# Query chunks with a deferred inversion, ten weight staging buffers, and reordered first tiles in a one-core graph transformer layer

## The reference

```
xn = layernorm(x)
deg = segment_sum(1, dst);  dinv = rsqrt(deg)
gnn = relu(segment_sum((xn @ W)[src] * dinv[src] * dinv[dst], dst) + b)
Q, K, V = xn @ Wq.T + bq, xn @ Wk.T + bk, xn @ Wv.T + bv     # 16 heads of 64
phiQ, phiK = elu(Q) + 1, elu(K) + 1
S = phiK^T V;  Z = sum(phiK)                                  # per head
mix = (phiQ S) / (phiQ Z + 1e-6) @ Wo.T + bo
x = x + gnn + mix
h = silu(xn2 @ w1.T * s1) * (xn2 @ w2.T * s2);  two gelu layers;  x = x + h @ w3.T * s3
```

## Time and profile before

| | |
|---|---|
| median of 3 runs | 1139.36 us (1137.54 to 1141.56) |
| the profiled execution | time 1137.78 us, span 1135.7 us |
| busy: PE, PEld, DVE, ACT, POOL | 1025.6, 853.8, 585.6, 289.7, 165.7 us |
| chain that ended last | PE 61%, DVE 17%, DMA 9%, ACT 4%, issue 4%, POOL 3% |
| mean granted TensorE clock | 0.953 |

### The profile page before, as it was taken

How to read it: one execution, slowest core, us unless ns; L and a number is a source line. 1 busy time by engine, 2 the same in 40 slices (tenths; PEclk the granted TensorE clock), 3 DMA queues, 4 the chain that set the end, 5 groups by cost and what they waited for, 6 DMA issues and landing times.

```text
span 1135.7 us, 13213 instructions
## 1 busy us (share of the span) xinstructions
PE 1025.6 (90%) x4932; PEld 853.8 (75%) x4932; DVE 585.6 (52%) x1074; ACT 289.7 (26%) x532; POOL 165.7 (15%) x208
## 2 busy tenths in 40 slices
PE   3779999998998979978989999788999997999998
PEld 2657888886878967856867785565877897999886
DVE  4766678666764776776137315752156510113354
ACT  5465213122124122121122113422013410125400
POOL 6010001001002013013040001000060005126200
PEclk9979999998998988987989999898999998999999
DMA  7120213102011012112335205643263201002043
GB/s 238 40 70 28 54 38 90 25 15 89 25 41 60 23 42 79 45 42 79 120 107 176 90 1 179 223 158 108 100 192 113 97 1 46 29 19 70 6 167 140
DMA packets 49405, 92.58 MB, mean 82 GB/s; under 512 B 16676, under 2 KB 20112, under 8 KB 49320
## 3 DMA queue, kind: packets, MB, share of 16 engines
q1 hardware_dynamic: 41640, 66.32, 17.7%
q0 software_dynamic: 7680, 25.17, 7.2%
HBM read 67.22 MB, written 23.76 MB: 80 GB/s over the span
## 4 chain that ended last, share of the span: by engine, by line
PE 61%; DVE 17%; DMA 9%; ACT 4%; issue 4%; POOL 3%; SPq 0%; DVEq 0%; POOLq 0%; ACTq 0%
PE PS L1198 8%; PE PS L1199 8%; PE PS L1200 8%; PE PS L1310 5%; PE PS L1311 5%; PE PS L1312 5%; DVE rec L1035 4%; PE PS L1237 3%; PE PS L1385 2%; PE PS L1384 2%; PE PS L1383 2%; POOL ring L355 2%; DMA phin_d<-phiq 2%; PE PS L1436 2%; PE PS L1437 2%
## 5 line engine op out<-in xcount | busy, mean ns | idle before, releaser
L1198 PE MATMUL PS<-ring,act_t 128*128 128x512 f32 (+1 forms) x480 | 199.6, 416 | 7.7 <-POOL ring L355 7.7
L1199 PE MATMUL PS<-ring,act_t 128*128 128x512 f32 (+1 forms) x480 | 193.5, 403 | 0.0
L1200 PE MATMUL PS<-ring,act_t 128*128 128x512 f32 (+1 forms) x480 | 193.4, 403 | 0.0
L1310 PE MATMUL PS<-act_t,ring 128*128 128x416 f32 (+1 forms) x432 | 163.7, 379 | 15.1 <-POOL ring L355 15.1
L1311 PE MATMUL PS<-act_t,ring 128*128 128x416 f32 (+1 forms) x432 | 155.0, 359 | 0.0
L1312 PE MATMUL PS<-act_t,ring 128*128 128x416 f32 (+1 forms) x432 | 154.2, 357 | 0.0
L1198 PEld LDWEIGHTS PS<-ring,act_t 128*128 128x128 f32 (+1 forms) x480 | 91.6, 191 | 33.6 <-POOL ring L355 11.8
L355 POOL TENSOR_TENSOR ring<-stage,ring 128x512 fp32r<-128x512 f32 x66 | 88.1, 1335 | 192.9 <-ACT ring L618 182.6
L1200 PEld LDWEIGHTS PS<-ring,act_t 128*128 128x128 f32 (+1 forms) x480 | 91.4, 190 | 23.5
L1199 PEld LDWEIGHTS PS<-ring,act_t 128*128 128x128 f32 (+1 forms) x480 | 91.8, 191 | 21.7 <-issue 0.9
L1310 PEld LDWEIGHTS PS<-act_t,ring 128*128 128x128 f32 x432 | 83.2, 192 | 24.5 <-POOL ring L355 20.1
(11 more groups left out here) (168 smaller groups left out, 1582.4 us busy)
## 6 DMA issues: line engine op xcount, KB each, us to landing
stage<-in_wslices_dram POOLq DMA_DIRECT2D x96, 256.0 KB, 2.9
xr<-x_d SPq DMA_DIRECT2D x27, 256.0 KB, 3.1
ctu<-ct_d SPq DMA_DIRECT2D x20, 320.0 KB, 3.2
phin_d<-phiq SPq DMA_DIRECT2D x8, 625.0 KB, 3.2
xrow<-in_x_dram SPq DMA_DIRECT2D x9, 512.0 KB, 3.5
xh<-in_x_dram SPq DMA_DIRECT2D x18, 256.0 KB, 2.5
x_d<-xh SPq DMA_DIRECT2D x18, 256.0 KB, 2.1
x_d<-xr SPq DMA_DIRECT2D x18, 256.0 KB, 2.1
```

The costliest lines, as they stand in the source:

```text
L1198: pe.matmul(out_ap, node_rows(0, k, t), ring[:, slot(k0 + k), 0, :], start=(k == 0), stop=False)
L1199: pe.matmul(out_ap, node_rows(1, k, t), ring[:, slot(k0 + k), 0, :], start=False, stop=False)
L1200: ins = pe.matmul(out_ap, node_rows(0, k, t), ring[:, slot(k0 + k), 1, :], start=False, stop=(k == KD - 1))
L1310: pe.matmul(out_ap, w[0], x_t[:, 0, k, o:o + n], start=(k == 0), stop=False)
```

## The change

It makes these edits:

- Six more staging buffers, `stage_x`, in memory that `wo_sb` and `ph_in` use later. Slices below 64 go round ten buffers, those from 64 on round four. SP waits until slice 63 is done before it loads `wo_sb`.
- The first two tiles: ScalarE takes the root of the second right behind the split of the first, and VectorE does the first tile's low part ahead of the second's inverse. `ln_finish` has one operation less, and its operations have one tensor input.
- Three windows in each of steps 10 to 36, and none after. `count_tile` moves behind the low halves of the weights. The sums of step 39 and the z units come after the first query unit, on TensorE and on ScalarE.
- Query chunks: the exp is written in place over `qmin`, `phiq` has three buffers, ScalarE reads the denominator out of PSUM and adds the constant (`den_copy`), TensorE does the denominator of chunk i-2, and VectorE's work is cut into `q_min`, `den_invert` (chunk i-3), `q_add` and `den_apply` (chunk i-3).
- `mix` waits for all 24 low parts of `ph` in place of 16.

```diff
-STAGE = 4
+PHI_BUFS = 3
+STAGE_A = 10
+STAGE_B = 4
...
-    u += [("z", i) for i in range(2)]
-    u += [("q", f, c) for f in range(KD) for c in range(3)]
+    u += [("q", 0, 0), ("z", 0), ("z", 1)]
+    u += [("q", f, c) for f in range(KD) for c in range(3) if f or c]
...
-    if 10 <= step < 40:
-        g, j = divmod(step - 10, 3)
-        return list(range(8 * g + 3 * j, 8 * g + min(3 * j + 3, 8)))
+    if 10 <= step < 37:
+        return list(range(3 * (step - 10), min(3 * (step - 9), NWIN)))
...
+        with ExitStack() as r1:
+            stage_x = sb("stage_x", [P, STAGE_A - STAGE_B, 512], F32, r1)
         wo_sb = sb("wo_sb", [P, WO_BUFS, 512], F32)
         ph_in = sb("ph_in", [P, PH_BUFS, 418], F32)
...
+        def stage_slot(n):
+            return n % STAGE_A if n < HI_ACT else n % STAGE_B
+
+        stage_uses = [[n for n in range(len(slices)) if stage_slot(n) == i] for i in range(STAGE_A)]
+
+        def stage_buf(n):
+            i = stage_slot(n)
+            return stage[:, i, :] if i < STAGE_B else stage_x[:, i - STAGE_B, :]
+
+        def loads_freed_by(n):
+            uses = stage_uses[stage_slot(n)]
+            i = uses.index(n) + 1
+            return uses[i:i + 1]
+
         def weight_hi(eng, copy, n):
             k = slices[n]
-            eng.wait_ge(stage_in[n % STAGE], 16 * (n // STAGE + 1))
+            i = stage_slot(n)
+            eng.wait_ge(stage_in[i], 16 * (stage_uses[i].index(n) + 1))
             if k >= RING:
                 wait_released(eng, k - RING)
-            copy(ring[:, slot(k), 0, :], stage[:, n % STAGE, :]).then_inc(w_hi, 1)
+            copy(ring[:, slot(k), 0, :], stage_buf(n)).then_inc(w_hi, 1)
...
+            sp.wait_ge(w_ready, HI_ACT)
...
+            for n in range(STAGE_A):
                 load(n)
...
-                if n + STAGE < len(slices):
+                for m in loads_freed_by(n):
                     pool.wait_ge(w_ready, n + 1)
-                    load(n + STAGE)
+                    load(m)
...
             transposed_hi(0)
-            for n in range(4, 10):
+            ln_root(1)
+            hi(4)
+            hi(5)
+            ln_apply(1)
+            for n in range(6, 10):
                 hi(n)
-                if n == 6:
-                    ln_root(1)
-                    ln_apply(1)
...
+            def sums_out():
+                act.wait_ge(s_done, sums_of(39))
...
+            def den_copy(i):
+                n = CHUNKS[i % 3][1]
+                act.wait_ge(den_done, i + 1)
+                if i >= 2:
+                    act.wait_ge(phin_ready, i - 1)
+                nc.scalar.activation(rec[:, i % 2, 0:n], PS[:, 3 + i % 2, 0:n], ACT.Identity,
+                                     bias=eps_sb).then_inc(den_read, 1)
...
+                nc.scalar.activation(qmin[:, i % 2, 0:n], qmin[:, i % 2, 0:n], ACT.Exp).then_inc(qact_ready, 1)
                 if i >= 2:
                     act.wait_ge(phiq_ready, i - 1)
-                nc.scalar.activation(qexp[:, i % 2, 0:n], qmin[:, i % 2, 0:n], ACT.Exp).then_inc(qact_ready, 1)
                 nc.scalar.activation(qrel[:, i % 2, 0:n], PS[:, bank(u), 0:n], ACT.Relu,
                                      bias=bq_sb[:, f:f + 1]).then_inc(acc_free[bank(u)], 1)
+                if i == 0:
+                    sums_out()
+                if i >= 2:
+                    den_copy(i - 2)
...
-                link(newton(c[0], c[1], c[2], c[3], c[5], c[4]))
-
-                dve.scalar_tensor_tensor(c[5], mv[0:r, i % 2, 0:1], -1.0, c[4], ALU.mult, ALU.mult).then_inc(rstd_ready, 1)
+                link(dve.reciprocal(y, root))
+                link(dve.tensor_scalar(t3, y, y, v, ALU.mult, ALU.mult))
+                link(dve.tensor_scalar(t3, t3, -0.5, 1.5, ALU.mult, ALU.add))
+                link(dve.tensor_scalar(out, y, t3, None, ALU.mult))
+
+                dve.tensor_scalar(shift, mv[0:r, i % 2, 0:1], out, -1.0, ALU.mult, ALU.mult).then_inc(rstd_ready, 1)
...
-            for i in range(2):
-                dve.wait_ge(x_in[i % 2], 16)
-                ln_stats(i)
-                ln_finish(i)
+            dve.wait_ge(x_in[0], 16)
+            ln_stats(0)
+            ln_finish(0)
+            dve.wait_ge(x_in[1], 16)
+            ln_stats(1)
+            transposed_lo(0)
+            ln_finish(1)
...
-                for dt in (tile_ended(step - 1) if step >= 1 else []):
-                    count_tile(dt, dve_more)
...
+                for dt in (tile_ended(step - 1) if step >= 1 else []):
+                    count_tile(dt, dve_more)
+                if step == 38:
+                    link(dve.tensor_reduce(cmx[:, 11:12], cmx[:, 0:NT], AX.X, ALU.max))
+                    dve.tensor_copy(cmx[:, 13:14], cmx[:, 11:12]).then_inc(cmx_ready, 1)
...
-                dve.tensor_tensor(phiq[:, f % 2, o:o + n], qexp[:, i % 2, 0:n], qrel[:, i % 2, 0:n],
...
-                dve.tensor_scalar(rec[:, i % 2, 0:n], PS[:, 3 + i % 2, 0:n], DEN_EPS, None, ALU.add).then_inc(den_read, 1)
...
+            def den_invert(i):
+                n = CHUNKS[i % 3][1]
                 dve.wait_ge(den_read, i + 1)
-                link(dve.reciprocal(rec[:, i % 2, 0:n], rec[:, i % 2, 0:n]))
-                dve.tensor_tensor(phiq[:, f % 2, o:o + n], phiq[:, f % 2, o:o + n], rec[:, i % 2, 0:n],
+                dve.reciprocal(rec[:, i % 2, 0:n], rec[:, i % 2, 0:n]).then_inc(rec_ready, 1)
+
+            def den_apply(i):
+                f, c = divmod(i, 3)
+                o, n = CHUNKS[c]
+                dve.wait_ge(rec_ready, i + 1)
+                dve.wait_ge(phiq_ready, i + 1)
+                dve.tensor_tensor(phiq[:, f % PHI_BUFS, o:o + n], phiq[:, f % PHI_BUFS, o:o + n], rec[:, i % 2, 0:n],
                                   ALU.mult).then_inc(phin_ready, 1)
             for i in range(24):
-                q_out(i)
+                q_min(i)
                 if i >= 3:
-                    den_out(i - 3)
+                    den_invert(i - 3)
+                q_add(i)
+                if i >= 3:
+                    den_apply(i - 3)
...
+            def key_sums():
+                kv_sum(39)
+                pe.wait_ge(consts, 2)
+                pe.wait_ge(ksum_ready, 40)
...
+                if i == 0:
+                    key_sums()
+                if i >= 2:
+                    denominator(i - 2)
...
-            pe.wait_ge(ph_lo, 2 * KD)
+            pe.wait_ge(ph_lo, 3 * KD)
```

119 lines of the change are left out of this document (52 added, 67 removed).

## The result

The changed kernel took 1105.23 us (median of 4 runs, 1104.43 to 1107.00), the kernel before 1139.2 (4 runs). The ratio is 0.9699 with a 95% interval of 0.9681 to 0.9717: faster, by 34 us where I had forecast 50.5. The time lies 2 us above the range of 1074 to 1103.

A forecast was written before the change was run, and what follows sets the result against it. TensorE was taken to carry the chain, with VectorE pacing the largest stage, the query stage, by 1.0 us a chunk. Terms summed to 50.5 us: 1137.8 - 50.5 = 1087.3, plus 1.6 for the median, so 1088; range 1074 to 1103.

The forecast's parts named there:

- Start: From the kernel's start to VectorE's read of the first key GEMM: read at 25.3 instead of 29.69, gain 4.4 us.
- Layer norm: Inverse root with one operation less: 1.4 us over seven tiles at 30 to 100 us, 0.7 in the final norm.
- Windows and count_tile: Key stage: TensorE's 4.61 us stall at step 29 and the low clock after it go; gain 5.7 us (3 to 6.2).
- Keys to queries: Passage from last key GEMM to second query unit: 7.8 us less a new wait, gain 6.8 (3 to 8).
- Query loop: Query stage: chunks go from VectorE's 6.25 us to TensorE's 5.25, store waits go; gain 25.7 us after slab-change losses.
- Slab changes: Two weight changes in the query stage: TensorE stalls 5.5 and 3.9 us, plus 1.5 lost to slow clock behind each.
- The rival that the loop keeps another bound: Query loop: VectorE or ScalarE stays over 5.25 us a chunk, total time 1112 or 1097; chance 0.20.
- The one that the weight waits go: Query stage: GpSimd is ahead at both slab changes, 12 us more gained, total time 1076; chance 0.10.
- After the marker: After the first G unit's end (519.77): one denominator less (0.7) and a slow start already counted (2.1), gain 2.8 us.
- Aggregation: Aggregation's start: 5.59 us TensorE stall shrinks, third unit starts at 14.0 instead of 17.6; gain 3.6 us (0 to 7).
- Port: VectorE operations with two SBUF inputs and GpSimd's subtractions hold each other up: 0.6 us lost, at most 7.
- its own signs of being wrong: VectorE still waiting for ScalarE each chunk, query-stage clock under 0.9, or aggregation's third unit waiting longer for ctu.

## Why the prediction was off, step by step

- **Start, 4.4.** Right in size (4.5), with a part that I had not seen: half of it hangs on the new inverse, which escapes GpSimd's subtractions. The third tile's load did come late (18.45) with six more loads beside it. It was hidden behind the low halves, but only just: with both sooner the first read moved to 24.48 in one run and to 23.74 in another.
- **Layer norm, 1.4 + 0.7.** Wrong step: "rows of it stand 0.19 apart", so one operation less saves 0.19. Three of the five that are left take 0.21 to 0.27 in their new form, and the chain is as long as before. From the first read to step 10 the changed kernel lost 1.0 where 1.4 was forecast (0.3 to 0.6 in eight other runs), half of it by the kmin beside the memset. The final norm gave 0.9 for 0.7 by luck: the gain is two tiles that escape GpSimd, not seven shorter chains.
- **Windows and count_tile, 5.7.** Step 29 went as forecast (steps 28 to 30 take 23.4 us for 29.3). The wrong step is "its degree matmul may wait 0.5": it waited 2.12 and cost 3.9 with the low clock behind it, as in this execution, and 2.4 without. I had given a price for the slow stretch and my new wait none.
- **Keys to queries, 6.8.** The new wait was seen and mis-sized, 2.62 for 1.0. That is 1.6 of the 2.2 missing there.
- **Query loop, 25.7.** Right: 24.9. The account of its parts was right in that the 17.1 us of store waits lay inside VectorE's bound; the third buffer and ScalarE's copy, to which I gave work in that sum, are worth nothing measurable. Slab changes: 9.4 + 3.0 forecast, some 13.4 lost (two units in 20.1 for 10.5, and 10.1 for 6.3 from the last qmin to the first G unit's end); other executions of the same loads lost up to 1.3 less. The rival that the loop keeps another bound did not come. The one that the weight waits go did not either, but it was one edit away.
- **After the marker, 2.8.** 1.4 by the end of the last G unit.
- **Aggregation, 3.6.** The step that failed. I had named SP's wait and the four loads behind it, and put the count load at 8.8 us issued, 12.7 landed, 14.0 used after the end of the last G unit. Measured: 10.4, about 16.2 and 17.7, where the third unit started at 17.6 before. The low half that SP waits for ended 8.4 after the G unit and not 7.0, 0.8 of that by one subtraction of 2.12 us beside VectorE's `clo`, and the load took 5.8 to land, not 3.9. Nothing was gained, and the unit then took 6.6 us for 4.6 (550 to 565 is granted 0.77). Together 5.7 short at that unit. Behind that I had let loads and stores pace the units "as now": the fourth count load stood behind an x load that waited for the store, and 2.4 more went by the tenth unit, 1.1 in the second half. That is 9.2 of the 19.6 us.
- **Port, -0.6.** Not separable in the changed kernel's query loop; where it bites is the start, the final norm and the low half that SP waits for.

The largest steps are thus shown by runs: the wo loads' place (4.6 of the span), the order of count and x loads, the count's place and the root's place. What is not settled is why one and the same wait at step 18 was followed by the low clock in some executions and not in others. The passage shows the same 1.5 us, and the query stage's first slab change differs by up to 1.3, which I put down to the same without having shown it.

The prediction also named its own signs of being wrong, and one of them came: the aggregation's third unit waits 6.58 us for its counts, and TensorE had no wait there before. The range was too narrow by its own method: I had added the terms' bounds as independent, and all but the start and the final norm missed to the same side.

## What to carry to other kernels

An in-order queue that only issues transfers is a resource like an engine: for each wait put into it, list what stands behind and what the first such item feeds, and put loads that something waits for ahead of loads that wait for a store. More buffers buy nothing at a place until the work that they make postponable there is in fact moved (here none at the query stage's slab changes, and 6 us or more at the first of them once the loads stood behind the subtractions); look for the issue between two computations. And of a change in several parts, find the one that is the gain: here one reordering, which puts the reciprocal where VectorE idled, gave by itself 27.7 us, of 34 for the whole. Write chains of tiny operations in a form that does not meet the engine beside them.

## What the runs showed of the hardware

- A wait of TensorE can cost more than its length, and not the same each time. 2.12 us at step 18 cost 3.9 in five of the eight executions that had it, with the low level behind it (granted 0.79 over 8 us), and 2.4 in three, at 1.00 throughout. 2.62 us in the passage cost 2.9 or 4.4. At the first slab change of the query stage 5.1 us cost 9.6, granted 0.74 over 20 us.
- On 128x1 operands a tensor_scalar with immediates takes 0.15 us, with one pointer operand 0.21, with two 0.27, a tensor_tensor 0.16.
- A two-input VectorE operation of 0.16 us that began in GpSimd's subtraction took 0.54 to 1.24, in a load issue alone 0.32, in a load issue with a subtraction behind it 1.64 to 1.75. A tensor_scalar of 128x1 was never held up; one of 128x256 took 0.75 for 0.29 beside GpSimd's memset.
- GpSimd's subtraction waits too: one of 1.28 us took 2.12 beside a VectorE operation of 1.48 with two inputs.
- A 320 KB count load took 3.4 us to land in the middle (3.0 with the new order), and 5.8 right behind four wo loads of 256 KB.
